# Two-layer graph attention on one core: the first layer's mask becomes a product with the identity, its minima and exponentials read PSUM, and every engine gets a new order

## What is computed

```
# layer 0, six heads of 64
q, k, v = heads(x @ Wq + bq), heads(x @ Wk + bk), heads(x @ Wv + bv)
scores  = q @ k.T / sqrt(64) + where(adj, 0, -9e15)
x       = layernorm(x + (softmax(scores) @ v) @ Wf + bf)
# layer 1, twelve heads of 32
h       = x @ W                      # per head
a       = tanh(h) @ w_src + (tanh(h) @ w_dst).T
a       = where(adj, leaky(a, 0.2), -999)
f       = elu(softmax(a) @ h + b)
gate    = sigmoid(x @ H_w.T + H_b)
x       = layernorm(x + gate * f + (1 - gate) * x)
```

## Time and profile before

| | |
|---|---|
| median of three runs | 1128.99 us |
| the profiled execution | 1128.99 us, of which 1126.7 us are its span |
| TensorE busy in the span | 1043.5 us (93%) |
| VectorE | 1024.0 us (91%) |
| ScalarE | 893.7 us (79%) |
| GpSimd | 947.8 us (84%) |
| mean granted TensorE clock | 0.975 of full speed |

### The profile page before, as it was taken

One profiled execution on the slowest core, in us unless ns is written; L12 is line 12 of the kernel. 1 busy time (PEld: TensorE's weight loads), 2 busy tenths in 40 slices (PEclk: granted clock), 3 DMA queues, 4 the chain that ended last, 5 costly groups with the idle time before them and its releaser, 6 DMA issues.

```text
span 1126.7 us, 32731 instructions
## 1 busy us (share of the span) xinstructions
PE 1043.5 (93%) x10827; PEld 951.1 (84%) x10890; DVE 1024.0 (91%) x2138; ACT 893.7 (79%) x1739; POOL 947.8 (84%) x781
## 2 busy tenths in 40 slices
PE   3899999999999999999999999999999999999761
PEld 3789998898989888888988988999888899988641
DVE  4579999999999999999999999999999999999954
ACT  4468888888888888888888888888888888888753
POOL 1148898888989988888998889899888898988785
PEclk8899999999999999999999999999999999999975
DMA  5013332323333332333433223333332343322232
GB/s 197 3 39 83 84 86 80 87 56 92 96 82 89 78 84 71 77 96 82 95 79 84 74 66 96 89 88 79 85 87 53 95 96 82 88 77 74 53 68 72
DMA packets 188716, 91.31 MB, mean 81 GB/s; under 512 B 158864, under 2 KB 183696, under 8 KB 188688
## 3 DMA queue, kind: packets, MB, share of 16 engines
q1 hardware_dynamic: 188688, 90.95, 32.3%
HBM read 31.61 MB, written 12.58 MB: 39 GB/s over the span
## 4 chain that ended last, share of the span: by engine, by line
PE 72%; issue 9%; DVE 8%; ACT 4%; POOL 4%; DMA 2%; SPq 1%; DVEq 0%; POOLq 0%; ACTq 0%
PE lin L459 42%; PE zp L557 6%; PE zp L613 3%; PE zp L617 3%; PE fp L583 3%; PE tp L498 3%; PE tp L567 3%; PE tp L626 2%; DVE sd L994 2%; PE tp L595 2%; PE fp L586 2%; PE fp L640 2%; ACT th L734 1%; ACT sd_t L763 1%; POOL z L1338 1%
## 5 line engine op out<-in xcount | busy, mean ns | idle before, releaser
L1338 POOL TENSOR_TENSOR z<-z,z_max 128x1536 f32<-128x1536 f32 x64 | 176.5, 2758 | 20.3 <-DVE z_max L1125 18.0
L816 ACT ACTIVATE z<-z,log_scale 128x1536 f32<-128x1536 f32 x64 | 101.3, 1583 | 53.4 <-POOL z L1338 53.4
L1345 POOL TENSOR_TENSOR p_lo<-z,p_hi 128x1024 f16<-128x1024 f32 x64 | 137.6, 2151 | 1.9 <-ACT p_hi L822 1.8
L1350 POOL TENSOR_TENSOR f<-f,x_kept 128x384 f32<-128x384 f32 x64 | 65.0, 1015 | 71.7 <-DVE f L1157 71.7
L1303 POOL TENSOR_TENSOR prod<-th,w_sd_rows 128x768 f32<-128x768 f32 x64 | 118.1, 1845 | 6.6 <-ACT th L734 6.3
L782 ACT ACTIVATE p<-p,p_min 128x128 f32<-128x128 f32 x384 | 119.0, 400 | 3.6 <-DVE p_min L1057 3.6
L1118 DVE SCALAR_TENSOR_TENSOR z<-zp,z 128x1536 f32<-128x1536 f32 x64 | 111.8, 1747 | 2.3 <-ACT z L791 2.3
L1125 DVE TENSOR_REDUCE z_max<-z 128x12 f32<-128x1536 f32 x64 | 111.5, 1743 | 0.1
L791 ACT ACTIVATE z<-zp 128x1536 f32<-128x1536 f32 x64 | 93.2, 1456 | 17.9 <-PE zp L617 17.9
L459 PE MATMUL lin<-xt_hi,Wq_hi 128*128 128x256 f32 x288 | 81.6, 283 | 19.3 <-POOL xt_lo L1321 12.8
L1316 POOL TENSOR_TENSOR v_part<-v_res,v_part 128x384 bf16<-128x384 f32 x64 | 63.0, 985 | 35.4 <-ACT v_part L753 33.2
(11 more groups left out here) (162 smaller groups left out, 4375.2 us busy)
## 6 DMA issues: line engine op xcount, KB each, us to landing
xt_raw<-x_t SPq DMA_DIRECT2D x32, 384.0 KB, 3.9
x_raw<-x SPq DMA_DIRECT2D x32, 384.0 KB, 3.2
...
dst_row<-sd_t SPq DMA_DIRECT2D x64, 9.0 KB
p1t_hi<-p_hi SPq DMA_TRANSPOSE x64, 3.2
p1t_lo<-p_lo SPq DMA_TRANSPOSE x64, 3.1
```

The costliest lines, as they stand in the source:

```text
L816: act.activation(z[:, g, :], z[:, g, :], ACT.Exp, bias=log_scale[:, :]).then_inc(z_exp[g].sem, 1)
L1338: pool.tensor_tensor(zs, zs, z_max[:, g, :].unsqueeze(2).to_broadcast([128, H1, N]), ALU.subtract)\
L1345: pool.tensor_tensor(p1_lo[:, g, :], z[:, g, PE_HEADS * N:], p1_hi[:, g, :], ALU.subtract).then_inc(w1_lo[g].sem, 1)
```

## The change

- `scores(g)` waits for mask0 and puts it into both halves' banks with two products of ident_bf and mask0 (384 columns each) before its own products, which then all accumulate.
- `scores_masked` and its signals are gone. `scores_min` reads PSUM, `scores_exp` reads PSUM and writes p0; it also takes over the wait for the transposes of the p0 before. A score bank is free only after `scores_exp`.
- `mask0_bias` waits for the score products of graph 1 instead of the masked sum.
- TensorE's list now begins with `queries_keys 2`, and the steps stand in another order; the bank users and their banks follow it. The lists of ScalarE, VectorE, GpSimd and SyncE are reordered too.

```diff
@@ -121,16 +121,16 @@
-LIN_USERS = ("h1", "g0", "qk0", "v0", "pr0", "g1", "pr1", "qk1", "qk2", "v1", "h0")
-TP_USERS = ("x1t1", "pt00", "pt01", "sdt", "pt10", "pt11", "ct0", "ct1", "wt0", "x1t0", "wt1")
-ZP_USERS = ("sc1", "z0", "z1", "sc0")
+LIN_USERS = ("qk2", "v1", "h0", "h1", "qk0", "g0", "v0", "pr0", "g1", "pr1", "qk1")
+TP_USERS = ("wt0", "x1t0", "x1t1", "wt1", "pt01", "pt00", "sdt", "pt10", "pt11", "ct0", "ct1")
+ZP_USERS = ("sc0", "sc1", "z0", "z1")
 FP_USERS = ("f0", "f1", "ctx0", "ctx1")
-LATE_USERS = ("h1", "g0", "pr0", "g1", "pr1", "x1t1", "pt00", "pt01", "sdt", "pt10", "pt11", "ct0", "ct1", "sc1", "z0", "z1", "f0", "f1", "ctx0", "ctx1")
-
-
-SECOND_BANK = ("g0", "v0", "pr1", "qk2", "h0", "x1t1", "pt01", "pt11", "ct0", "ct1", "wt0")
+LATE_USERS = ("qk2", "v1", "h0", "h1", "g0", "pr0", "g1", "pr1", "wt0", "x1t0", "x1t1", "wt1", "pt01", "pt00", "sdt", "pt10", "pt11", "ct0", "ct1", "sc0", "sc1", "z0", "z1", "f0", "f1", "ctx0", "ctx1")
+
+
+SECOND_BANK = ("qk2", "h0", "h1", "g0", "v0", "pr1", "x1t0", "x1t1", "sdt", "pt10", "ct1")
 def bank_of(user):
@@ -276,7 +276,7 @@
...
-        sc_mm, sc_masked = pair_of("sc_mm", 0), pair_of("sc_masked", 0)
+        sc_mm = pair_of("sc_mm", 0)
...
@@ -323,7 +323,7 @@
...
-                            f"sc{g}": sc_masked[g], f"z{g}": z_leaky[g], f"ctx{g}": ctx_ready[g],
+                            f"sc{g}": sc_exp[g], f"z{g}": z_leaky[g], f"ctx{g}": ctx_ready[g],
...
@@ -430,19 +430,19 @@
                     turn.apart()
                     sp.dma_start(out_d[turn.pair(2), :, g, :], out_tile[:, g, :]).then_inc(stored[g].sem, 16)
-                turn.late(1, keep_x1, 0)
-                turn.late(-1, load_x)
                 turn.step(-1, load_transposed_x)
+                turn.step(-1, load_adj0)
                 turn.late(1, turn_weights1_high, 0)
-                turn.late(1, keep_x1, 1)
                 turn.late(1, turn_weights1_low, 0)
+                turn.late(1, turn_weights1_low, 1)
                 turn.late(1, turn_weights1_high, 1)
                 turn.late(0, load_adj1)
-                turn.late(1, turn_weights1_low, 1)
-                turn.step(-1, load_adj0)
+                turn.step(1, targets_flat)
+                turn.late(-1, load_x)
                 turn.late(2, store, 0)
-                turn.step(1, targets_flat)
                 turn.late(2, store, 1)
+                turn.step(1, keep_x1, 0)
+                turn.step(1, keep_x1, 1)
             for g in range(2):
@@ -549,13 +549,17 @@
                     bank_free(ZP_USERS, f"sc{g}")
                     for j in range(C):
                         pe.wait_ge(qk_lo[j].sem, now(qk_lo[j]))
+                    pe.wait_ge(mask0_ready.sem, now(mask0_ready))
+                    for half in range(2):
+                        pe.matmul(zp[:, half, 0:C * N], ident_bf[:, :], mask0[:, g:g + 1, :].to_broadcast([128, C, N]),
+                                  start=True, stop=False, skip_group_check=True)
                     own = slice(N * g, N * (g + 1))
                     for j in range(C):
                         for i, (q, k) in enumerate(((q_hi, k_hi), (q_hi, k_lo), (q_lo, k_hi))):
                             for half in range(2):
                                 p = slice(64 * half, 64 * half + 64)
                                 last = pe.matmul(zp[:, half, N * j:N * (j + 1)], q[p, j, own], k[p, j, own],
-                                                 start=(j == 0 and i == 0), stop=(i == 2), skip_group_check=True)
+                                                 start=False, stop=(i == 2), skip_group_check=True)
                     last.then_inc(sc_mm[g].sem, 1)
                 def weights0_transposes(g, half):
@@ -643,26 +647,33 @@
                     if k == 2:
                         last.then_inc(f_mm[g].sem, 1)
+                turn.late(0, queries_keys, 2)
+                turn.late(2, weights1_transposes, 0)
+                turn.late(1, x1_transposes, 0)
+                turn.late(0, values, 1)
+                turn.late(0, scores, 0)
+                turn.late(1, hidden, 0)
                 turn.late(1, x1_transposes, 1)
-                turn.late(0, scores, 1)
                 turn.late(2, attend1, 0, 0)
+                turn.late(2, weights1_transposes, 1)
                 turn.late(2, attend1, 0, 1)
                 turn.late(2, attend1, 0, 2)
                 turn.late(1, hidden, 1)
-                turn.late(0, weights0_transposes, 0, 0)
+                turn.late(0, scores, 1)
                 turn.late(0, weights0_transposes, 0, 1)
-                turn.late(1, gate_rows, 0)
                 turn.step(0, queries_keys, 0)
                 turn.late(2, attend1, 1, 0)
                 turn.late(2, attend1, 1, 1)
+                turn.late(2, attend1, 1, 2)
+                turn.late(0, weights0_transposes, 0, 0)
                 turn.late(1, source_target_transposes)
-                turn.late(2, attend1, 1, 2)
+                turn.late(1, gate_rows, 0)
                 turn.late(0, weights0_transposes, 1, 0)
+                turn.late(0, attend0, 0)
                 turn.late(0, weights0_transposes, 1, 1)
-                turn.late(0, attend0, 0)
                 turn.late(1, attention1, 0)
+                turn.late(0, attend0, 1)
                 turn.late(0, context_transposes, 0)
-                turn.late(0, attend0, 1)
                 turn.step(0, values, 0)
                 turn.late(0, project, 0)
                 turn.late(0, context_transposes, 1)
@@ -670,13 +681,6 @@
                 turn.late(1, gate_rows, 1)
                 turn.late(0, project, 1)
                 turn.step(0, queries_keys, 1)
-                turn.step(0, queries_keys, 2)
-                turn.step(2, weights1_transposes, 0)
-                turn.step(1, x1_transposes, 0)
-                turn.step(0, values, 1)
-                turn.step(0, scores, 0)
-                turn.step(1, hidden, 0)
-                turn.step(2, weights1_transposes, 1)
@@ -778,8 +782,11 @@
                 def scores_exp(g):
                     act.wait_ge(sc_min[g].sem, now(sc_min[g]))
+                    for half in range(2):
+                        act.wait_ge(pt_mm[half][g].sem, prev(pt_mm[half][g]))
                     for h in range(H0):
-                        last = act.activation(p0[:, g, N * h:N * (h + 1)], p0[:, g, N * h:N * (h + 1)], ACT.Exp,
+                        last = act.activation(p0[:, g, N * h:N * (h + 1)],
+                                              zp[:, h // C, N * (h % C):N * (h % C + 1)], ACT.Exp,
                                               bias=p0_min[:, g, h:h + 1], scale=-1.0)
                     last.then_inc(sc_exp[g].sem, 1)
@@ -849,46 +856,46 @@
...
                 turn.late(1, z_exponent, 1)
+                turn.late(1, weights1_high, 1)
+                turn.late(0, norm0, 1)
                 turn.step(-1, next_x_high)
+                turn.step(1, hidden_tanh, 0)
+                turn.step(1, x1_high, 1)
                 turn.step(0, value_part1, 1)
-                turn.late(0, norm0, 1)
-                turn.step(1, hidden_tanh, 0)
+                turn.step(0, scores_exp, 0)
                 turn.step(2, turned1_high, 1)
-                turn.step(1, x1_high, 1)
-                turn.late(1, weights1_high, 1)
-                turn.step(0, scores_exp, 0)
+                turn.late(1, gate_quarter, 1)
                 turn.step(1, hidden_tanh, 1)
-                turn.step(0, weights0_high, 0, 0)
+                turn.late(2, norm1, 0)
                 turn.step(0, weights0_high, 0, 1)
                 turn.step(0, scores_exp, 1)
-                turn.late(2, norm1, 0)
-                turn.late(1, gate_quarter, 0)
                 turn.step(2, elu_exp, 0)
+                turn.step(0, value_part2, 1)
+                turn.step(0, weights0_high, 0, 0)
+                turn.step(1, source_target_copy)
                 turn.step(1, hidden_part1, 0)
-                turn.step(1, source_target_copy)
-                turn.late(1, gate_tanh, 1)
-                turn.step(0, value_part2, 1)
+                turn.late(2, norm1, 1)
                 turn.step(0, weights0_high, 1, 0)
+                turn.step(2, elu_exp, 1)
                 turn.step(0, weights0_high, 1, 1)
-                turn.step(2, elu_exp, 1)
-                turn.late(1, gate_quarter, 1)
-                turn.late(2, norm1, 1)
@@ -1036,25 +1043,15 @@
...
-                def scores_masked(g):
+                def scores_min(g):
                     if turn.starts(0) and g == 0:
                         projection_bias()
                         hidden_unit()
-                    dve.wait_ge(mask0_ready.sem, now(mask0_ready))
                     dve.wait_ge(sc_mm[g].sem, now(sc_mm[g]))
-                    for half in range(2):
-                        dve.wait_ge(pt_mm[half][g].sem, prev(pt_mm[half][g]))
-                    dve.tensor_tensor(p0[:, g, :].rearrange("p (b a n) -> p b a n", b=2, a=C),
```

(68 more changed lines are left out.)

20 lines of the change are left out of this document (13 added, 7 removed).

## The result

The changed kernel takes 1155.26 us (median of four runs, 1154.89 to 1155.36) against 1128.78 us for the kernel before on the same chip: a ratio of 1.0227, with a 95% interval of 1.0214 to 1.024. It is 26.5 us slower, nearly twice the 14.7 us that were forecast. Its profiled span is 1153.5 us, 26.8 more than before; the mean granted clock is 0.975 in both.

What follows compares the result with a forecast made beforehand. TensorE was taken to set the turn, VectorE close behind. 32 turns at +0.46 us gave +14.7, start and end 0: 1126.7 + 14.7 = 1141.4 us of span, plus 2.3 outside it, 1143.7, called 1143; range 1124 to 1160.

Steps and rivals of the forecast that it cites:

- Mask products, 0.64 per turn: Four added 384-column products on TensorE at 0.161 us each: 0.64 us per turn, from above 0.86 with changes of kind.
- Rival (d), the faster stream: Mask products on TensorE stream faster, 0.39 us per turn for 0.64, giving 1135 us; chance 0.04.
- Two holes, 0.65 removable: TensorE's waits per turn: 0.24 us for sd_parts before sdt, 0.41 at the PSUM bank sdt shares with pt10; both removable.
- my sum for TensorE alone: TensorE's own content of a turn: 32.64 - 0.65 + 0.64 + 0.09 + 0.15 = 32.87 us.
- The loop through sdt, 32.97: Chain from second-layer scores 1 through GpSimd and VectorE to sdt and back to scores; needs 32.97 us per turn.
- 33.1: Forecast turn in us: the sdt loop's 32.97 plus 0.1 for other near steps; 0.46 more than before.
- SyncE and GpSimd at nothing: Reordered loads and stores, load_x behind targets_flat, cost nothing; GpSimd's 9% idle time would cover a wait of raise_x.
- Start and end 0, ends -4 and +5: Filling and draining: saved VectorE pass -0.95 at two or three places, start wait +2, masks at lower clock +0.5; taken as 0.
- Exponentials 380 ns, minimum 940 to 953: Time per operation on ScalarE (exponentials, 400 ns before) and VectorE (minimum, 940 ns before) once they read PSUM.
- The bank covered by 0.7 us: Scores' PSUM bank free 4.5 us after scores 0, while TensorE has 5.2 us of other work before scores 1.
- rival (c): Graph 0's exponentials start late and scores 1 waits on its bank; 0.5 us late each turn gives 1159; chance 0.14.
- Rival (b), faster: VectorE's dropped work closes more TensorE gaps and split groups cost nothing: turn 32.33 us, 1119 us; chance 0.20.

Runs made afterwards that it cites:

- a_half_low_sums: Changed kernel with half of graph 1's second-layer low weights left out on GpSimd and VectorE's source_target_sums 1 ahead of weights0_low (0,1): 1151.19 us.
- b_product_mask: Kernel before with the mask products, minima and exponentials from PSUM and the later bank release, every list in its old order: 1313.27 us, ratio 1.1613.

## Why the prediction was right, and where its steps were off

The sign, the main cause (TensorE takes over what VectorE drops) and the wide range held: 1155.3 in 1124 to 1160. The size did not: forecast 1143, with an own range of 1136 to 1152, so the result lies outside what I called my forecast, and only the width of the stated range took it in. Of the 12 us between, 3.9 are start and end, forecast at 0, and 8.2 are the turns, forecast at +14.7 and measured at +22.9.

- **Mask products, 0.64 per turn.** Mis-sized: 0.84 measured from block to block, and the stated upper bound of 0.86 was right. The pitch was right (0.165 for 0.161); the change of kind, which I put only into the upper bound, is real with 64-row scores behind it. +6.4 us over 32 turns. Rival (d), the faster stream, falls with 0.165 us.
- **Two holes, 0.65 removable.** The 0.41 at the bank went (attend1 with it -0.55). The 0.24 for sd_parts did not: it is 0.27. In my sum for TensorE alone I took it off and named the loop through GpSimd for it; `a_half_low_sums` shows that it hangs behind TensorE's scores 1. With both terms mended, 32.87 becomes 33.34, close to the 33.30 of a quiet turn; partly by chance, for the 0.20 that TensorE waits for x has no term in it.
- **The loop through sdt, 32.97.** It exists and was well sized: 33.04 where mask products are gone. But it was not what set the turn, and that 33.1 got over half of the size from it is luck: with its two terms right, TensorE's content (33.34) would have stood above this loop. Had it been the bound, doubling the mask products would not have cost their full price.
- **SyncE and GpSimd at nothing.** Wrong. load_x behind targets_flat makes GpSimd wait 1.5 us a turn, and its 9% of idle time did not cover that, since it lies elsewhere in the turn (2 us of it before v_part, `POOL v_part L1311`). By the turns above it costs 3.5 us, and it makes a loop through the load that the prediction does not have.
- **Start and end 0, ends -4 and +5.** It is +3.2 before the first sdt and +0.7 after the last, near the upper end. The forecast wait of some 3 us of scores 1 came as 2.75, and two others came with it; TensorE's waits between 30 us and the first sdt sum to 8.4 us, before to 5.8, so the saved VectorE passes do not show as a gain:

```profile
38.85 0.82 PE L554 MATMUL zp<-mask,ident_bf 128*128 128x384 bf16 x2 [2.75 <-ACT p L788]
...
69.10 0.42 PE L459 MATMUL lin<-W_hi,x1t_hi 128*128 128x384 f32 x1 [1.42 <-DVE h_res L986]
...
76.89 0.28 PE L529 MATMUL tp<-ident_bf,sd_parts 128*128 128x128 bf16 x2 [1.62 <-DVE sd_parts L1023]
```
- **Exponentials 380 ns, minimum 940 to 953.** 388 and 955; VectorE 90.7%, forecast near 90.
- **The bank covered by 0.7 us.** Right in the steady turn: graph 0's exponentials end at 571.09, 0.61 before the mask products of scores 1 (571.70); TensorE waits for them nowhere but at the start. So rival (c) did not come, though its 1159 us is nearer than the forecast. `b_product_mask` shows what that cover was worth.
- **Rival (b), faster.** It needed over 0.64 us back per turn; 0.55 and some small pieces came back, against 0.84 and the split groups.
